# The last expert layer fed by gathers: finding the token of every slot with mask products instead of scattering rows into a queue

## The reference, cut to what matters

```
logits = x @ router_w + router_b ; probs = softmax(logits)      # 4096 tokens, E = 8
topv, topi = top_k(probs, 2) ; topv = topv / topv.sum(-1)
prio = where(flat_i == e, flat_v, -1)                           # per expert, over 2 x 4096 entries
pv, pp = top_k(prio, capacity)                                  # capacity = 768
tok = pp // 2 ; w = pv
xin = x_flat[tok]                                               # 8 x 768 rows are picked
h = gelu(xin @ w1[e] + b1[e]) ; out_e = (h @ w2[e] + b2[e]) * w # 128 -> 512 -> 128
out = zeros.at[tok].add(out_e) ; out = layer_norm(out) * ln_g + ln_b
x = x + out
```

## Time and profile before

| | |
|---|---|
| time, median of 3 runs | 2843.49 us (2841.66 to 2847.01) |
| profiled execution | 2844.36 us, span 2842.4 us |
| busy share of the span | PE 76%, DVE 63%, PE weight load 53%, ACT 45%, POOL 42% |
| mean granted TensorE clock | 0.875 of full speed |
| `router3` and `experts3` | from 2498 us to the end, 344 us |

### The profile page before, as it was taken

The page is one execution under the profiler, slowest core; times in us unless marked ns, Lnnn a source line. Parts: engine busy times, 40 slices in busy tenths (PEclk is TensorE's granted clock), DMA queues, the critical chain, the costliest instruction groups (busy, mean ns, idle before and its releaser), DMA issues. The chain is left out here.

```text
span 2842.4 us, 46464 instructions
## 1 busy us (share of the span) xinstructions
PE 2173.5 (76%) x15040; PEld 1506.1 (53%) x15040; DVE 1797.3 (63%) x4896; ACT 1292.6 (45%) x2803; POOL 1193.5 (42%) x1166
## 2 busy tenths in 40 slices
PE   1799999999998678339389996959999999841290
PEld 0466666566667567227245554845555666530180
DVE  3677777776875757301367773748889888943023
ACT  1445454545443237213235553736666666430143
POOL 1424242333421100545422121557777777704453
PEclk9899999999999659569679996979999999955595
DMA  6500000000002000112233331000000000000123
GB/s 202 141 1 0 0 0 0 0 0 0 0 1 67 0 0 1 38 52 73 77 101 84 83 104 53 0 1 1 0 0 0 0 0 0 0 0 29 50 63 96
DMA packets 105972, 93.81 MB, mean 33 GB/s; under 512 B 12380, under 2 KB 92406, under 8 KB 105718
## 3 DMA queue, kind: packets, MB, share of 16 engines
q1 hardware_dynamic: 98198, 76.85, 9.7%
q0 software_dynamic: 7680, 15.81, 1.7%
HBM read 62.15 MB, written 46.26 MB: 38 GB/s over the span
## 5 line engine op out<-in xcount | busy, mean ns | idle before, releaser
L3182 POOL TENSOR_SCALAR mb_w<-mb_duT,mb_bT 128x256 f32<-128x256 f32 x512 | 467.9, 932 | 116.7 <-PE bank L3192 85.3
L3117 DVE TENSOR_TENSOR_SCAN mb_hs<-mb_dA,bank 128x512 f32<-128x512 f32 x256 | 300.8, 1205 | 34.6 <-issue 25.0
L38 POOL TENSOR_TENSOR scrap<-ones 128x1 f32<-128x1 f32 x64 | 12.5, 195 | 694.1 <-DVE gla_ss L420 486.8
L3211 PE MATMUL bank<-mb_hc,ident 128*128 128x512 f32 x512 | 256.1, 624 | 15.7 <-DVE mb_hc L3127 15.4
L3173 ACT ACTIVATE mb_dA<-mb_delta,mb_A 128x255 f32<-128x255 f32 x512 | 216.4, 495 | 8.4 <-DVE mb_hs L3117 8.2
L2339 DVE TENSOR_REDUCE ra_mx<-bank 128x2 f32<-128x512 f32 x256 | 163.6, 686 | 57.4 <-PE bank L2193 54.9
L2429 ACT ACTIVATE ra_pT<-bank 128x512 f32<-128x512 f32 x256 | 141.1, 600 | 114.1 <-PE bank L2215 113.8
L1924 ACT ACTIVATE e_hid<-bank,e_b 128x512 f32<-128x512 f32 (+1 forms) x128 | 81.2, 634 | 214.2 <-PE bank L1965 211.3
L3192 PE MATMUL bank<-ident,mb_w 128*128 128x128 f32 x1024 | 150.0, 280 | 34.3 <-DVE mb_hs L3117 26.3
L1885 POOL DMA_INDIRECT results<-e_y,e_x x112 | 109.1, 974 | 144.1 <-DVE e_y L2000 119.1
L1957 PE MATMUL bank<-ident,e_x 128*128 128x128 f32 x112 | 18.8, 292 | 189.2 <-DMA e_x<-queue 189.2
(11 more groups left out here) (529 smaller groups left out, 6160.3 us busy)
## 6 DMA issues: line engine op xcount, KB each, us to landing
results<-const_empty SPq DMA_DIRECT2D x2, 4096.0 KB
e_got<-results SPq DMA_DIRECT2D x32, 256.0 KB, 3.4
rope_rows<-ra_part SPq DMA_DIRECT2D x48, 128.0 KB, 1.9
ra_k<-rope_rows SPq DMA_DIRECT2D x32, 192.0 KB, 3.3
ra_q<-rope_rows SPq DMA_DIRECT2D x32, 192.0 KB, 4.1
queue<-const_spare_rows SPq DMA_DIRECT2D x1, 4128.0 KB
e_x<-queue SPq DMA_DIRECT2D x8, 516.0 KB, 4.3
e_w<-in_L_ffn_w SPq DMA_DIRECT2D x2, 2048.0 KB, 8.1
```

The source lines that it names most:

```text
L3117: dve.tensor_tensor_scan(hs[n // 2 % 2][:, n % 2, :, :].rearrange("p c t -> p (c t)"), dA[n % RD][:, :, :].rearrange("p c t -> p (c t)"), ...
L3182: ins = pool.tensor_scalar(w[n % RH][:, h, :], duT[k][:, h, :], bT[k][:, h, n:n + 1], None, ALU.mult)
L3211: ins = pe.matmul(YB[:, :], g.ident[:, :], hc[grp % 2][:, j, :, :].rearrange("p c t -> p (c t)"), start=(n == 0), stop=(n == NS - 1))
```

## The change

For the last layer alone (`by_weight` / `last`):

- The router no longer scatters. SP writes the normalised rows to a table `rows3` in HBM in token order, four DMAs of 1024 rows of 128 values, as ACT finishes them. The 64 scatters and ACT's copy of the rows are gone.
- The slot number of each of the 64 columns is split on DVE into `low` (slot mod 128) and `high` (slot / 128, 0 to 47). `is_low` (128 x 128 for each column, bf16) and `is_high` (128 x 48) compare them with a row of numbers `iota`. `named` holds `is_high` times (tile number + 1) (DVE) and `is_high` times the token's place in its tile (ACT). PE sums `is_low`^T @ `named` over the 64 columns in PSUM, which gives a table with one place for each of the 6144 slots: which token sits there. DVE makes `g.source` (row of `rows3`) and `g.target` (row of `results3`) from it; unused slots get a trash row.
- In the experts, SP loads nothing. Pool gathers each half's three tiles from `rows3` with three indirect DMAs. It gathers six halves ahead (`AHEAD`) before its first scatter; then it alternates: three scatters of half u, three gathers of half u+6. `XR` is 4.
- `iota` is loaded in `load`; the initial fill of `queue3` (3096 KB) is dropped.

```diff
@@ router
+    if by_weight:
+        ROWS = 16
+        is_low = [sb(f"is_low{q}", [P, ROWS, P], BF16) for q in range(4)]
+        is_high, named = sb("is_high", [P, 2 * NTILE, SLOTS], BF16), sb("named", [P, 2 * NTILE, 2, SLOTS], BF16)
...
+            dve.wait_ge(slots_ready, 2)
+            every = places[:, :, :].rearrange("p k t -> p (k t)")
+            dve.tensor_scalar(parts2[:, 0, :], every, 7, None, ALU.logical_shift_right)
+            step(dve.tensor_scalar(parts2[:, 1, :], every, P - 1, None, ALU.bitwise_and))
+            dve.tensor_copy(high[:, :], parts2[:, 0, :])
+            step(dve.tensor_copy(low[:, :], parts2[:, 1, :]))
+            for q in range(4):
+                if q % 2 == 0:
+                    at = slice(q * ROWS, (q + 2) * ROWS)
+                    dve.tensor_tensor(is_high[:, at, :], g.iota[:, 0:SLOTS].unsqueeze(1).broadcast_to([P, 2 * ROWS, SLOTS]),
+                                      high[:, at].unsqueeze(2).broadcast_to([P, 2 * ROWS, SLOTS]), ALU.is_equal)\
+                        .then_inc(high_ready, 1)
+                at = slice(q * ROWS, (q + 1) * ROWS)
+                dve.tensor_tensor(is_low[q][:, :, :], g.iota[:, :].unsqueeze(1).broadcast_to([P, ROWS, P]),
+                                  low[:, at].unsqueeze(2).broadcast_to([P, ROWS, P]), ALU.is_equal).then_inc(low_ready, 1)
+                dve.wait_ge(high_ready, q // 2 + 1)
+                dve.tensor_tensor(named[:, at, 0, :], is_high[:, at, :],
+                                  g.iota[:, q * ROWS + 1:(q + 1) * ROWS + 1].unsqueeze(2).broadcast_to([P, ROWS, SLOTS]),
+                                  ALU.mult).then_inc(tile_named, 1)
+            own = g.ids[:, :, :].rearrange("p k t -> p (k t)")[:, 0:SLOTS]
+            dve.tensor_scalar(trash[:, :], own, float(RESULTS + P), None, ALU.add)
+            dve.wait_ge(table_psum, 1)
+            step(dve.tensor_scalar(named_as[:, :], cnt_bank[:, 0:SLOTS], float(P), -float(P), ALU.mult, ALU.add))
+            step(dve.tensor_tensor(named_as[:, :], named_as[:, :], cnt_bank[:, SLOTS:2 * SLOTS], ALU.add))
+            dve.scalar_tensor_tensor(out=empty[:, :], in0=named_as[:, :], scalar=-0.5, in1=trash[:, :],
+                                     op0=ALU.is_lt, op1=ALU.mult)
+            step(dve.tensor_scalar(token[:, :], named_as[:, :], TOKENS - 0.5, -float(TOKENS), ALU.is_ge, ALU.mult))
+            dve.tensor_tensor(empty[:, :], empty[:, :], named_as[:, :], ALU.add)
+            step(dve.tensor_tensor(token[:, :], token[:, :], named_as[:, :], ALU.add))
+            step(dve.tensor_scalar(token[:, :], token[:, :], 0.0, None, ALU.max))
+            dve.tensor_copy(g.source[:, :], token[:, :])
+            step(dve.tensor_copy(g.target[:, :], empty[:, :]))
...
+                for q in range(4):
+                    sp.wait_ge(kept0, 4 * q + 4)
+                    sp.dma_start(g.rows3[q * 8 * P:(q + 1) * 8 * P, :].rearrange("(t p) c -> p t c", p=P),
+                                 rows[0].rearrange("p (t c) -> p t c", c=ROW)[:, q * 8:q * 8 + 8, 0:P])\
+                        .then_inc(kept_rows, 16)
+                sp.wait_ge(kept_rows, 64)
...
+            for q in range(4):
+                pe.wait_ge(low_ready, q + 1)
+                pe.wait_ge(tile_named, q + 1)
+                pe.wait_ge(row_named, q // 2 + 1)
+                for r in range(ROWS):
+                    at = q * ROWS + r
+                    ins = pe.matmul(cnt_bank[:, 0:2 * SLOTS], is_low[q][:, r, :],
+                                    named[:, at, :, :].rearrange("p a s -> p (a s)"), start=(at == 0),
+                                    stop=(at == 4 * ROWS - 1))
+            ins.then_inc(table_psum, 1)
@@ experts
-    XR, YR = 3, 4
+    XR, YR = (4, 4) if last else (3, 4)
...
+            def gather(u):
+                e, half = u // 2, u % 2
+                if e >= XR:
+                    pool.wait_ge(t_psum, u - 2 * XR + 1)
+                for t in range(half * HT, (half + 1) * HT):
+                    at = e * TILES + t
+                    pool.indirect_dma_start(
+                        out=x[e % XR][:, t, 0:P], out_offset=None, in_=g.rows3[:, :],
+                        in_offset=bass.IndirectOffsetOnAxis(ap=g.source[:, at:at + 1], axis=0))\
+                        .then_inc(half_loaded[half][e % XR], 16)
+
+            AHEAD = 6
+            if last:
+                for u in range(AHEAD):
+                    gather(u)
             for u in range(N):
...
+                if last and u + AHEAD < N:
+                    gather(u + AHEAD)
...
-                pe.wait_ge(x_loaded[e % XR], 16 * (e // XR + 1))
+                if last:
+                    pe.wait_ge(half_loaded[half][e % XR], 16 * HT * (e // XR + 1))
+                else:
+                    pe.wait_ge(x_loaded[e % XR], 16 * (e // XR + 1))
```

More of the change, by code:

```diff
@@ L104, in constants @@
     c["ids"] = ids
+    c["iota"] = np.broadcast_to(np.arange(P), (P, P))
     c["empty"] = np.zeros((P, P))
@@ L1481, in router @@
     ok, spare = sb("ok", [P, NTILE]), sb("spare", [P, 2, NTILE])
-    slot = [sb(f"slot{k}", [P, NTILE], U32) for k in range(2)]
+    slot = [places[:, k, :] for k in range(2)] if by_weight else [sb(f"slot{k}", [P, NTILE], U32)[:, :] for k in range(2)]
     cum_banks, tot_banks, cnt_bank = (g.pb[4], g.pb[6]), (g.pb[5], g.pb[7]), g.pb[3]
@@ L1511, in _ @@
             dve.tensor_scalar(var[:, :], moments[:, :, 1], LN_EPS, None, ALU.add).then_inc(var_ready, 1)
-            for k in range(2):
+            for k in range(len(rows) if not by_weight else 0):
                 dve.tensor_copy(row_ids(k), g.ids[:, k, :])
@@ L1745, in _ @@
             act.wait_ge(kept0, NSEQ)
+            if by_weight:
+                for q in range(2):
+                    act.wait_ge(high_ready, q + 1)
+                    at = slice(q * 2 * ROWS, (q + 1) * 2 * ROWS)
+                    act.activation(named[:, at, 1, :], is_high[:, at, :], ACT.Copy, scale=g.ids[:, 0, 0:1])\
+                        .then_inc(row_named, 1)
+                return
             for q in range(NSEQ // 4):
@@ L1826, in experts @@
     func = ACT.Gelu if last else ACT.Relu
-    x_loaded, sent = sig("xl", XR), [nc.alloc_semaphore(f"{name}_sent{k}") for k in range(YR)]
+    x_loaded, half_loaded = sig("xl", XR), [sig(f"xh{h}", XR) for h in range(2)]
+    sent = [nc.alloc_semaphore(f"{name}_sent{k}") for k in range(YR)]
     t_psum, xT_ready, y_psum, y_ready = sig("tp"), sig("xT"), sig("yp"), sig("y")
@@ L1854, in _ @@
         def _(sp):
-            for e in range(E_N):
+            for e in range(0 if last else E_N):
                 if e >= XR:
@@ L1884, in _ @@
                 for t in range(HT):
-                    pool.indirect_dma_start(
-                        out=results[:, :], in_=y[u % YR][:, t, :], in_offset=None,
-                        out_offset=bass.IndirectOffsetOnAxis(
-                            ap=x[e % XR][:, half * HT + t, P:ROW].bitcast(U32), axis=0)).then_inc(sent[u % YR], 16)
+                    at = e * TILES + half * HT + t
+                    to = g.target[:, at:at + 1] if last else x[e % XR][:, half * HT + t, P:ROW].bitcast(U32)
+                    pool.indirect_dma_start(out=results[:, :], in_=y[u % YR][:, t, :], in_offset=None,
+                                            out_offset=bass.IndirectOffsetOnAxis(ap=to, axis=0))\
+                        .then_inc(sent[u % YR], 16)
+                if last and u + AHEAD < N:
+                    gather(u + AHEAD)
             def joined(i):
@@ L2088, in router3 @@
 def router3(nc, g):
-    router(nc, g, "r3", g.r3_w, g.r3_b, True, CAP3, g.queue3)
+    router(nc, g, "r3", g.r3_w, g.r3_b, True, CAP3, None)
 def experts3(nc, g):
-    experts(nc, g, "e3", g.e3_w1, g.e3_b1, g.e3_w2, g.e3_b2, True, CAP3, g.queue3, g.results3)
+    experts(nc, g, "e3", g.e3_w1, g.e3_b1, g.e3_w2, g.e3_b2, True, CAP3, None, g.results3)
 RH, HD = 16, 8
@@ L3492, in program @@
         g.g_ffn = column("g_ffn", ins["L0_attn_g_ffn"])
-        g.ids = const("ids")
+        g.ids, g.iota = const("ids"), const("iota")
         g.first, g.loads = g.loads, []
@@ L3546, in program @@
         g.b_out = row("b_out", ins["L3_attn_b_out"])
-        for to, rows in ((g.queue1, E_N * CAP1), (g.queue3, E_N * CAP3)):
+        for to, rows in ((g.queue1, E_N * CAP1),):
             g.loads.append(tuple(a[0:rows, :].rearrange("(p j) c -> p (j c)", p=P) for a in (to, consts["spare_rows"])))
```

17 lines of the change are left out of this document (15 added, 2 removed).

## The result

| | kernel before | kernel after |
|---|---|---|
| median of 15 runs | 2843.75 us (2836.11 to 2852.59) | 2825.78 us (2818.05 to 2835.95) |
| ratio after/before | | 0.9934, 95% interval 0.9921 to 0.9947 |
| profiled execution / its span | 2844.36 / 2842.4 us | 2828.28 / 2826.2 us |

The change makes the kernel 18 us faster. I had forecast 38. The direction was right, but less than half of the size came.

What follows compares the result with a forecast made beforehand. Pool's scatters alone bound the router's end and PE the experts; after the change Pool would bound the experts. 20.5 + 2.8 + 126.1 = 149.4 us replace 190.0; less 2.2, 38.4 us saved: 2805 us, range 2786 to 2826.

Steps and rivals of the forecast that it cites:

- (e): Pool in the last experts: 96 indirect DMAs at 1.265 us plus waits, 126.1 us, making Pool the bound.
- (a): Last router, masks on DVE: 14336 elements at about 0.0010 us each plus ten operations' fixed cost, 15.4 us.
- (c): Last router, DVE's tail: nine operations of 48 columns with five waits one after another, 1.6 us.
- (d): End of the last router: no 5.27 us Pool drain left; clearing semaphores and engines meeting take 2.8 us.
- behind the last scatter: Results read back, sum, norm and store after the last scatter's issue: taken as unchanged, 0 us.
- (f): Other stages: the `iota` load adds 0.5 us and 21 more semaphores 1.7 us, 2.2 us in all.
- (b): Last router, PE and ACT beside the masks: only the last matmul group and its hand-over count, 2.8 us.
- rival 1: Experts: gathers cost more to issue than scatters; at 1.7 us each the kernel takes 2826 us; chance 0.12.
- Rival 2: Experts: PE's clock stays at half speed, PE becomes the bound, 2872 us; chance 0.05, shared with other 40 us causes.
- Rival 3: Experts: DVE's copies from PSUM also hold Pool by the lock, 16 us more, 2821 us; chance 0.06.
- Rival 4: Experts: gathers overlap far better, so PE is the bound, 2787 us; chance 0.12, shared with cheaper gathers.

Runs made afterwards that it cites:

- c1_after: The kernel after, unchanged, run again on a chip where nothing crawls: 2805.32 us (4 runs), ratio 0.9866 to the kernel before.
- d1_after: The kernel after, unchanged, run a third time, on a chip where it crawls: 2822.87 us (5 runs), ratio 0.9922 to the kernel before.
- f1_after: The kernel after, unchanged, run on another chip without crawling: 2812.92 us (one run), beside 2845.02 of the kernel before.

## Why the prediction was wrong, point by point

**The step that failed is the overlap in (e).** I took PE's 89 us of work and Pool's 121 us of issues as running side by side with neither slowing the other, but for 2.4 us at L2004, and gave anything beyond that no term. In the first profile PE fell behind beside Pool's pause-free row, Pool then waited for `e_y` 23 us in all, and the stage took 144.4 us instead of 126.1. A second, smaller term was put at nothing without a reason: the end of the block, 4.1 us.

Term by term, with the crawling execution of the first profile and that of `c1_after` without crawling (us):

| step | forecast | first profile | `c1_after` |
|---|---|---|---|
| (a) to (c): last slots to DVE's end | 20.5 | 19.8 | 19.8 |
| (d) end of the router | 2.8 | 3.5 | 3.5 |
| (e) Pool's part of the experts | 126.1 | 144.4 | 125.3 |
| sum, in place of 190.0 | 149.4 | 167.6 | 148.6 |
| behind the last scatter, more than before | 0 | 4.1 | 4.1 |
| (f): stages ahead, more than before | 2.2 | 2.0 | -2.3 |
| span saved, of 2842.4 | 38.4 | 16.2 | 39.5 |

- **(a) masks: right.** 15.6 us from 2593.92 to 2609.55, forecast 15.4. 0.0010 us for each element held at 2048 elements too (2.28 us).
- **(b) last PE group: too dear.** 1.65 us from DVE's last mask to its next operation, forecast 2.8. A weight load at half clock and its matmul of 96 columns go by in 0.09 us a pair (16 in 1.44).
- **(c) tail: right**, 1.7 us against 1.6.
- **(d): right.** No drain of 5 us stands before the experts; Pool had gone through it from 2500.7 on, over 100 us before its first DMA. 3.5 against 2.8 us.
- **(e) is right in its prices, and wrong in its overlap.** The gather's issue took 0.95 us and the next began 1.25 us later, so the price I could not see in the trace was right, and rival 1 is out. Without crawling Pool's additions came to 3.9 us (125.3 less 96 x 1.265), forecast 4.7: no wait at the start instead of 1 us, and 0.5 us for each of seven DMAs that begin beside L2100 (L2004 before; 1.36 to 1.51 us instead of 0.96), which I had at 0.3. One of them in `c1_after`:

```profile
2654.46 0.68 DVE L2100 TENSOR_TENSOR x<-x,l_ln_b 128x512 f32<-128x512 f32 x1
2654.53 1.45 POOL L1977 DMA_INDIRECT results<-e_y,target  x1 [0.30 <-issue]
```

  The scatter of the earlier trace rows and these seven follow one rule: the DMA is longer by what is left of DVE's operation when it begins, less 0.1 us (0.61 us left, 0.49 longer here; 0.32 left, 0.19 longer there). So my 0.19 was the price of a late start, and the 0.68 us by the Trainium skill (SBUF — State Buffer, section SBUF: two separate sides), which has the loser blocked until the other is done, is nearer. The page gives this block to an operation with two SBUF inputs only against a GpSimd instruction that reads SBUF, and it reports a probe in which `tensor_tensor`, which L2100 is, did not stall DMAs. Here it does. Then crawling adds 15.8 us (`d1_after`) to 19.1 us (first profile). No row of before could show it: in that trace Pool's long row of DMAs had no PE work beside it, and the scatters beside PE had a pause in each half. My rivals asked whether Pool or PE would be slower by their own work, and not whether one could disturb the other.
- **Behind the last scatter I took everything as unchanged, and that is wrong by 4 us.** The drain at the end of `experts3` is 3.9 us longer with 96 DMAs than with 48. Rows of before held it: 5.30 us for 48 and 6.60 for 64.
- **(f): not told apart.** The last slots are ready 2.0 us later than before in the first profile, beside a forecast of 2.2, but 2.3 us earlier in `c1_after` and 5.7 us later in `f1_after`: the stages ahead vary by more than that.
- **Rival 2, the clock: out.** In `c1_after` the last 61 us run at 0.95 with a gap of 1.9 us in each half. Where the clock fell in the first profile, crawling came first: at 2636 to 2642 the clock is 1.00 and PE does 10 matmuls in 6 us.
- **Rival 3, copies from PSUM holding Pool: out.** Only DMAs beside L2100 were longer. **Rival 4: out**, Pool is the bound of the kernel after where it does not crawl (it waits 0.9 us for results in `c1_after`, 0.6 in `f1_after`).

So the unchanged kernel, repeated on three chips, gave the forecast of 2805.0 us within 8 us on two (2805.3 with four runs, 2812.9 with one). That 2805.3 is so close is partly luck: the 4.1 us behind the last scatter, which I had not counted, are offset by stages ahead that ended 2.3 us earlier instead of 2.2 us later. The first 15 runs (2825.8) and `d1_after` (2822.9) are 18 to 21 us above. The profile of the first shows crawling; of the other 14 there is no trace, and that they crawl too is read from their times alone. They end at the upper edge of my range, which I had kept for dearer gathers; the gathers were not dearer.

**What is shown and what is not.** Shown: the crawling costs what is missing, but for the 4.1 us behind the last scatter; it does not come with the file alone, which crawls in one place and not in another; scatters bring it as gathers do; the kernel before, with 48 scatters in the stage and a pause in each half, takes the same time in both places (2844.79 and 2846.84 us), so it pays nothing there that can be told; pauses of Pool lessen it, by one trace with and one without; and the five traced executions that crawl also lack the landings of Pool's DMAs, in earlier stages too, where nothing crawls. Not shown is what connects these. The lost records suggest a path for records or semaphore events that is slower on such a chip and fills up when Pool's DMAs (three in 3.8 us, each raising its semaphore by 16) and PE's short instructions come together. This is a guess. The Trainium skill (NOTIFIC — the notification-queue block, section Overflow: three behaviours, one of which stalls the engine) states that the block which writes such records can, in one of its modes, hold back an engine when its queue is full. No run here shows that: all executions timed here carry a clock and a span, and so were recorded, and one without records wasn't tried. If that is the cause, an unrecorded execution would not crawl. Bytes and the number of PE's instructions as conditions stay open as well, and so does whether the kernel before with PE at work beside its 64 scatters would crawl in such a place.

No version tried here that computes the whole layer beats the kernel after: four halves ahead and the paced one are slower without crawling, eight halves ahead and the paced one are no faster with it.

## What to carry to other kernels

Moving work to an engine that had idle time is priced well by count times pitch (96 x 1.265 us held to 4 us where nothing crawled), but the moved work also fills the pauses, and a row of before with pauses in it says nothing about the engines beside once they are gone. The end of `experts` has a price that grows with the DMAs issued in it, so look at what ends a block too. And when a profile shows idle time that nothing accounts for ("issue", "remote"), run the unchanged kernel again elsewhere before you look for the cause in its code: here the same file gave 2805.3 and 2822.9 us.

## What the hardware showed that I had not expected

- PE's instructions 0.7 or 1.4 us apart with their data ready, up to 15.5 us from the end of PE's work (2661.87) to DVE's start on it (2677.38), in the first profile and on one chip of the experiments, and on three other chips not at all.
- Pool's drain at the end of `experts`: 5.30 us after 48 indirect DMAs, 6.60 after 64, 9.22 after 96, though the issue of the last scatter had ended 52.6 us ahead of it (first profile), where a scatter lands in 2.3 us (`c1_after`).
- A DVE operation with two inputs in SBUF holds back a Pool DMA, gather or scatter, that begins beside it, by what is left of the operation less 0.1 us: 0.40 to 0.55 us of 0.68.
- A gather of 128 rows of 512 bytes takes 0.95 us to issue and lands 2.5 us after issue (scatter 2.3), and a quarter of the bytes changes neither the pitch nor, by more than 0.2 us, the landing (2.4 and 2.1).
